# A decoder layer on one core: projections as three short passes, routed sums in DRAM, scatter in tiles of 128 rows

## What is computed

```python
# 1. mixer: running sums over the tokens
out = (a_b * c_b @ U_b.T + alpha * (a_t * z_t * c_t) @ U_t.T) / counts + bias;  x = x + out @ Wo.T
# 2. cross attention, 16 heads of 32 features
Q = x @ Wq.T                         # (224, 512)
K, V = split(ctx @ Wkv.T)            # two times (750, 512), contraction over 256
x = x + softmax(Q K.T * scale) V @ Wo.T
# 3. expert choice: 32 experts, each picks its 8 best tokens of every batch
vals, idx = top_k(softmax(x @ gate_w.T, over tokens), 8)
merged = sum_k x[idx_k] * vals_k                     # one row per batch and expert
o = gelu([merged, 1] @ w1[e]) ; o = [o, 1] @ w2[e]   # 512 -> 2048 -> 512
x = x.at[idx].add(o * vals)                          # scattered back to the tokens
```

## Time and profile before

| | us |
|---|---|
| three runs | 2379.69, 2379.73, 2370.84 (median 2379.69) |
| profiled execution | 2371.13 |
| its span | 2369.5 |
| TensorE busy | 1953.3 |
| VectorE busy | 974.9 |
| ScalarE busy | 754.6 |
| GpSimd busy | 826.8 |

### The profile page before, as it was taken

How to read it: one execution, slowest core, us unless ns; L and a number is a source line. 1 busy time by engine, 2 the same in 40 slices (tenths; PEclk the granted TensorE clock), 3 DMA queues, 4 the chain that set the end, 5 groups by cost and what they waited for, 6 DMA issues and landing times. The chain is left out here.

```text
span 2369.5 us, 39997 instructions
## 1 busy us (share of the span) xinstructions
PE 1953.3 (82%) x11970; PEld 1146.6 (48%) x11970; DVE 974.9 (41%) x2477; ACT 754.6 (32%) x1551; POOL 826.8 (35%) x592
## 2 busy tenths in 40 slices
PE   7789999999999999999999999986755655655633
PEld 5466666666666666666666666653211111111101
DVE  0355655656556556565565565651100000000003
ACT  2143434435444344354443443532100000000000
POOL 0245545555555455555554555543000000000000
PEclk8899999999999999999999999987877777777765
DMA  5223333242233332422433324263999999999974
GB/s 159 56 74 93 77 87 84 72 101 64 74 94 78 86 84 72 102 64 72 96 77 83 84 73 103 65 227 115 370 423 419 421 422 420 423 420 420 422 261 136
DMA packets 135414, 419.34 MB, mean 177 GB/s; under 512 B 32612, under 2 KB 74820, under 8 KB 110804
## 3 DMA queue, kind: packets, MB, share of 16 engines
q1 hardware_dynamic: 130292, 410.08, 50.9%
q10 hardware_dynamic: 4096, 7.80, 1.0%
q0 software_dynamic: 992, 1.02, 0.1%
HBM read 306.39 MB, written 16.15 MB: 136 GB/s over the span
## 5 line engine op out<-in xcount | busy, mean ns | idle before, releaser
L1035 DVE TENSOR_REDUCE maxes<-bank 112x1 f32<-112x376 f32 (+1 forms) x1024 | 506.8, 538 | 208.8 <-PE bank L1240 208.1
L863 ACT ACTIVATE probs<-bank 125x448 f32<-125x448 f32 x768 | 402.8, 546 | 360.4 <-PE bank L1262 353.2
L1262 PE MATMUL bank<-q_st,k_st 98*125 98x224 f32 x1536 | 384.3, 339 | 15.6 <-DMA q_st<-max_lo 9.1
L739 POOL TENSOR_TENSOR psum_keys<-psum_keys,probs 125x896 f32<-125x896 f32 x128 | 269.0, 2102 | 312.3 <-ACT probs L863 307.0
L1600 PE MATMUL bank<-ring,hid_T 128*32 128x512 f32 x1024 | 181.9, 875 | 204.3 <-DMA ring<-in_L_ffn_w 201.1
L1240 PE MATMUL bank<-k_st,q_st 96*112 96x376 f32 (+1 forms) x1024 | 324.7, 370 | 16.3 <-DVE maxes L1035 7.2
L1262 PEld LDWEIGHTS bank<-q_st,k_st 98*125 98x125 f32 x1536 | 265.6, 192 | 127.4 <-issue 74.7
L742 POOL TENSOR_TENSOR psum_keys<-psum_keys,probs 125x896 f32<-125x896 f32 x128 | 267.5, 2089 | 10.0
L1515 DVE TENSOR_TENSOR o_fin<-bank,b_row 16x512 f32<-16x512 f32 x32 | 21.7, 679 | 588.4 <-PE bank L1558 588.4
L1438 POOL DMA_DIRECT2D o_rows<-o_fin x31 | 15.3, 495 | 595.6 <-DVE o_fin L1515 595.6
L1240 PEld LDWEIGHTS bank<-k_st,q_st 96*112 96x112 f32 x1024 | 165.5, 180 | 80.5 <-DVE maxes L1035 45.4
(11 more groups left out here) (149 smaller groups left out, 2250.5 us busy)
## 6 DMA issues: line engine op xcount, KB each, us to landing
ring<-in_L_ffn_w SPq DMA_DIRECT2D x128, 2048.0 KB, 30.5
k_st<-k_hi SPq DMA_DIRECT2D x512, 93.8 KB, 2.2
k_st<-k_lo SPq DMA_DIRECT2D x256, 93.8 KB, 2.2
q_st<-q_hi SPq DMA_DIRECT2D x512, 28.0 KB, 1.8
ctx_nat<-in_ctx SPq DMA_DIRECT2D x16, 750.0 KB
x_in<-in_x SPq DMA_DIRECT2D x16, 448.0 KB, 3.6
q_st<-q_lo SPq DMA_DIRECT2D x256, 28.0 KB, 1.9
out<-x SPq DMA_DIRECT2D x16, 448.0 KB, 7.9
```

The lines of the kernel that those rows point to most:

```text
L739: nc.gpsimd.tensor_tensor(psum_keys[:], psum_keys[:], lo, ALU.add).then_inc(pool_chain, 1)
L863: nc.scalar.activation(probs[n % 2][:, j, :], bank[5 + u % 2][0:SK, 0:2 * T], ACT.Exp, scale=SCALE).then_inc(probs_ready, 1)
L1035: nc.vector.tensor_reduce(maxes[:, j, t, c:c + 1], bank[2 + n % 3][0:TT, 0:SC[c + 1] - SC[c]], AX.X, ALU.max).then_inc(s_drained, 1)
L1262: last = nc.tensor.matmul(bank[5 + u % 2][0:SK, kk * T:(kk + 1) * T], k_st[slot][:, j, k * SK:(k + 1) * SK], q_st[slot][:, j, :], start=Tr ...
```

## The change

1. *Projections.* Context and Wkv are kept as an fp32r tile with the rounded value and one with the rest: `wk_hi`, `wk_lo`, `wv_hi`, `wv_lo`, `ctx_hi`, `ctx_lo`. Each k and v job makes six fp32r matmuls (high by high, high by low, low by high, for two halves of the contraction) in place of two fp32 ones. `ctx_hi` is ScalarE's copy as before; `ctx_lo` is a new subtraction on VectorE, and it, not the copy, now frees the bank. In the setup VectorE makes four such subtractions, and TensorE waits for them before it reuses those banks.
2. *Routed sums.* `mt` turns 112 rows in place of 128; its result goes into a small tile `m_now` and is stored in `routed` in DRAM by one DMA per batch (`keep_routed`), and read back as one DMA at the end of the attention stage. `merged_T` and `b1_rows` now lie in the memory of V (`late`), so that the loads of the expert biases come later too, after the last multiplication by V. Some other tiles share memory.
3. *Scatter.* `out` is seen as 28 tiles of 128 rows. A tile may span two batches and then is the sum of two matmuls. `picks` is loaded by four DMAs, with zeros around each batch's columns. `o_rows` is read back in two parts: experts 0 to 15 before `out` is read, and 16 to 30 after the last weights. `out` is read by four DMAs of 128 partitions, and each tile is stored by a DMA of its own.

```diff
-                        nc.scalar.copy(ctx_T[:, kc, half * 3 * SK:(half + 1) * 3 * SK],
-                                       ps[:, 0:3 * SK]).then_inc(s, 1)
+                        nc.scalar.copy(ctx_hi[:, kc, half * 3 * SK:(half + 1) * 3 * SK],
+                                       ps[:, 0:3 * SK]).then_inc(ctx_hi_ready, 1)
...
+                    elif job[:2] == "ct":
+                        kc, cols = i % 2, slice(i // 2 * 3 * SK, (i // 2 + 1) * 3 * SK)
+                        dve.wait_ge(work_full, full)
+                        dve.wait_ge(ctx_hi_ready, bb * 4 + (i + 1))
+                        nc.vector.tensor_tensor(ctx_lo[:, kc, cols], ps[:, 0:3 * SK],
+                                                ctx_hi[:, kc, cols].bitcast(F32), ALU.subtract
+                                                ).then_inc(s, 1)
...
+                        terms = [(wk_hi, ctx_hi), (wk_hi, ctx_lo), (wk_lo, ctx_hi)]
                         for kc in range(KC):
-                            last = nc.tensor.matmul(ps[:, 0:SC[c + 1] - SC[c]],
-                                                    wk_T[:, kc, kt * P:(kt + 1) * P],
-                                                    ctx_T[:, kc, chunk(c)], start=(kc == 0),
-                                                    stop=(kc == KC - 1))
+                            for n, (w, z) in enumerate(terms):
+                                last = nc.tensor.matmul(ps[:, 0:SC[c + 1] - SC[c]],
+                                                        w[:, kc, kt * P:(kt + 1) * P],
+                                                        z[:, kc, chunk(c)],
+                                                        start=(kc == 0 and n == 0),
+                                                        stop=(kc == KC - 1 and n == 2))
...
+                def keep_routed(b):
+                    b = value(b)
+                    sp.wait_ge(mt_ready, b + 1)
+                    sp.dma_start(routed[b] if isint(b) else routed[bass.ds(b, 1)].rearrange(
+                        "o p n -> p (o n)"), m_now[:].rearrange("p k e -> p (k e)")
+                                 ).then_inc(m_stored, 16)
+
+                def recall_routed():
+
+                    sp.wait_ge(pv_done, 12 * B)
+                    expert_biases()
+                    sp.wait_ge(m_stored, 16 * B)
+                    sp.dma_start(merged_T[:, 0:LAST].rearrange("p b k e -> p b (k e)"),
+                                 routed[0:LAST].rearrange("b p n -> p b n")
+                                 ).then_inc(routed_loaded, 16)
...
                         if kt == 3 and kind != "first":
                             keep_weight(b - 1)
+                        if kt == 3 and kind != "first":
+                            keep_routed(b - 1)
...
-                for b in range(B):
-                    if b % RW == 0:
-                        sp.wait_ge(h_full if b < B // 2 else o_full, E - 1)
-                    sp.dma_start(fin(b), out[b, :, :].rearrange("(p t) d -> p t d", p=TT)
-                                 ).then_inc(fin_loaded[b // RW], 16)
+                sp.wait_ge(o_stored, 16 * (E - 4))
+                for r in range(RW):
+                    read_back(r, 0, E // 2)
+                for g in range(-(-NT // PER)):
+                    sp.wait_ge(h_full if g < 2 else o_full, E - 1)
+                    n = min(PER, NT - g * PER)
+                    sp.dma_start(ring[:, g, 0:n * D].rearrange("p (k d) -> p k d", d=D),
+                                 rows_out[:, g * PER:g * PER + n, :]).then_inc(fin_loaded[g], 16)
                 weights(end, 1, False, (2, 3))
                 sp.wait_ge(o_stored, 16 * (E - 1))
                 for r in range(RW):
-                    sp.dma_start(o_in[r * E:(r + 1) * E - 1, :, :],
-                                 o_rows.rearrange("(g r) e n -> r e g n", r=RW)[r, 0:E - 1, :, :]
-                                 ).then_inc(o_loaded, 16)
+                    read_back(r, E // 2, E - 1)
...
+                for cycle in range(GB):
+                    scatter(0, 0, True, True)
+                    scatter(1, 1, True, False)
+                    scatter(3, 2, True, False)
+                    scatter(5, 3, True, False)
+
+                    scatter(2, 1, True, True)
+                    scatter(4, 2, True, True)
+                    scatter(6, 3, True, True)
+
+                    scatter(1, 0, False, True)
+                    scatter(3, 1, False, True)
+                    scatter(5, 2, False, True)
```

More of the change, by code:

```diff
@@ L137, in build @@
         o_rows = nc.dram_tensor("o_rows", [B, E, D], F32).ap()
+        routed = nc.dram_tensor("routed", [B, P, KD * E], F32).ap()
         ident = sb(es, "ident", [P, P])
-        merged_T = sb(es, "merged_T", [P, KD, E, B])
-        b1_rows = sb(es, "b1_rows", [P, BANK])
+        late = sb(es, "late", [P, NK * D])
+        wv_lo = sb(es, "wv_lo", [P, KC, D], F32R)
+        merged_T = late[:, 0:B * KD * E].rearrange("p (b k e) -> p b k e", b=B, k=KD)
+        b1_rows = late[:, B * KD * E:B * KD * E + BANK]
         b1_loaded = sem("b1_loaded")
@@ L260, in build @@
             needs[len(flips)] = "kv"
-            for h, dst in ((0, wk_T), (1, wv_T)):
+            KV0 = len(flips)
+            kv_lo = []
+            for h, dst, lo in ((0, wk_hi, wk_lo), (1, wv_hi, wv_lo)):
                 for i in range(KC):
@@ L343, in _ @@
                     pe.wait_ge(s_out, n - 7)
+                    lo_taken(pe, n)
                     pe.wait_ge(s_cnt, 2)
@@ L1353, in build @@
         o_in = sb(es, "o_in", [P, GB, D])
-        picks = sb(es, "picks", [P, GB, T])
+        LEAD = [r * T % P for r in range(RW)]
+        picks = sb(es, "picks", [P, GB, LEAD[1] + T + 64])
         b1_flipped = sem("b1_flipped")
@@ L1377, in build, with fin, drained, tile_at @@
         fin_stored = sem("fin_stored")
-        def fin(b):
-            return ring[0:TT, b // RW, b % RW * 2 * D:(b % RW + 1) * 2 * D].rearrange(
-                "p (t n) -> p t n", t=2)
+        NT = B * T // P
+        PER = 2 * H // D
+        rows_out = out.rearrange("b t d -> (b t) d").rearrange("(k p) d -> p k d", p=P)
+        def fin(k):
+            return ring[:, k // PER, k % PER * D:(k % PER + 1) * D]
+        CYCLE = RW * T // P
+        TURN = [0, 2, 4, 6, 1, 3, 5]
+        def drained(k):
+            return k // CYCLE * CYCLE + TURN.index(k % CYCLE) + 1
+        def tile_at(n):
+            return n // CYCLE * CYCLE + TURN[n % CYCLE]
         with nc.Block() as block:
@@ L1414, in _, with read_back @@
                 weights(end, 1, False, (0, 1))
-                for b in range(B):
-                    if b % RW == 0:
-                        sp.wait_ge(h_full if b < B // 2 else o_full, E - 1)
-                    sp.dma_start(fin(b), out[b, :, :].rearrange("(p t) d -> p t d", p=TT)
-                                 ).then_inc(fin_loaded[b // RW], 16)
+                def read_back(r, e0, e1):
+                    sp.dma_start(o_in[r * E + e0:r * E + e1, :, :],
+                                 o_rows.rearrange("(g r) e n -> r e g n", r=RW)[r, e0:e1, :, :]
+                                 ).then_inc(o_loaded, 16)
+                sp.wait_ge(o_stored, 16 * (E - 4))
+                for r in range(RW):
+                    read_back(r, 0, E // 2)
[4 more added lines that the diff above has]
+                                 rows_out[:, g * PER:g * PER + n, :]).then_inc(fin_loaded[g], 16)
                 weights(end, 1, False, (2, 3))
@@ L1469, in _ @@
                     hidden(i, 1, False)
-                for b in range(B):
-                    act.wait_ge(fin_ready, 2 * b + 2)
-                    act.dma_start(out[b, :, :].rearrange("(p t) d -> p t d", p=TT), fin(b)
-                                  ).then_inc(fin_stored, 16)
-                act.wait_ge(fin_stored, 16 * B)
+                for n in range(NT):
+                    k = tile_at(n)
+                    act.wait_ge(fin_ready, n + 1)
+                    act.dma_start(rows_out[:, k, :], fin(k)).then_inc(fin_stored, 16)
+                act.wait_ge(fin_stored, 16 * NT)
             @block.vector
@@ L1611, in _, with scatter @@
                 sum_parts(E // 2 - 1, 1, False)
-                pe.wait_ge(picks_loaded, 16)
-                pe.wait_ge(o_loaded, 16 * (RW + GB))
-                for g in range(GB):
-                    for t in range(2):
-                        for r in range(RW):
-                            if g:
-                                pe.wait_ge(fin_ready, (g - 1) * 2 * RW + 2 * r + t + 1)
-                            rows = slice(r * E, (r + 1) * E)
-                            nc.tensor.matmul(bank[t * RW + r][0:TT, :],
-                                             tokens(picks[rows, g, :], t), o_in[rows, g, :],
-                                             start=True, stop=True).then_inc(scat_full, 1)
+                pe.wait_ge(picks_loaded, 16 * RW)
```

(14 more changed lines are left out.)

110 lines of the change are left out of this document (68 added, 42 removed).

## The result

The changed kernel takes 2406.77 us (median of four runs, 2405.45 to 2415.48); the kernel before, run beside it on the same chip, 2379.09 us. The ratio of the means of the runs is 1.0132, with a 95% interval of 1.0099 to 1.0165 (that of the two medians is 1.0116): slower by 1.3%, against 1.007 forecast (2397 over 2379.7). The profiled execution took 2405.45 us, with a span of 2403.8 us and a mean granted clock of 0.893.

The account below looks back on a forecast made before the run. It took SyncE's queue (q0 to xt0), then TensorE, to bound attention batches, with DMA and a one-engine read-back later. 2371.1 +31 +9 +1 -1 +15 -2.6 -27 -3 gave 2393; half the run spread made 2397 us, range 2375 to 2420.

Parts of the forecast that it names:

- signs: Listed trace marks, among them batches of 97 to 98 us, longer x_in waits, clock under 1.00, scatter 13 us after weights.
- The clock: Attention batches: TensorE falls to 1.2 GHz after waits, two falls in five batches, 1 us a batch, +15 us (0 to 39).
- rival 3: Attention batches: the clock falls in every batch for its full price, 2417 us, up to 2440; chance 0.15.
- ctx low parts: Context transposes: ct2 waits for VectorE's subtraction of ct0, 2.06 us a batch, 15 times, +31 us.
- The routed store: SyncE's queue ahead of load_x: one more DMA a batch, 0.65 us, 14 times, +9 us.
- The short passes: Key and value jobs, q0 to xt0: 72 us less TensorE time, costed at zero gain.
- SyncE's queue: Attention batch, first copy after q0 to xt0: queue of copies and loads sets 55.9 us, TensorE almost equal.
- Rival 1: Attention batches: TensorE is the bound after all, so the passes' 72 us come in, 2306 us; chance 0.17.
- Read-back: End: o_rows' second half on 15 partitions spreads over engines, scatter 13 us after weights, not 40.2; -27 us.
- the scatter: End: 28 adds in place of 32 and faster, earlier stores, -3 us (0 to -5).
- Rival 4: End: transfers to 15 partitions stay on one engine, +14, 2407 to 2411 us; chance 0.06.
- Reading `out`: Late stage: 128-partition reads 5.6 us less, o_rows ahead of the last weights 2.9 more, -2.6 us (-5 to +3).

Follow-up runs that it names:

- fp32_again: Changed kernel with each key and value job back to one fp32 product of the high parts, low parts still computed; 2395.6 us.
- fp32_no_ct_low: Changed kernel without the context's low parts, each key and value job one fp32 product of the high parts; 2350.2 us.
- no_ct_low: Changed kernel without VectorE's subtractions for the context's low parts; the second short pass takes the high part again; 2349.2 us.
- x_early_no_ct_low: Changed kernel with the load of x early and without the context's low parts, the high part's product added twice; 2309.8 us.
- raw_first: Changed kernel, arithmetic kept, ScalarE first copying the first context transpose's whole bank to SBUF to free it early; 2377.3 us.
- one_pass: Changed kernel with one short pass (high by high) in each key and value job instead of three; 2452.2 us.
- raw_x_early: Changed kernel, arithmetic kept, with the first context bank freed early through a copy and the load of x early; 2330.4 us.

## Why the prediction was right or wrong

**Verdict and size.** 2397 was said and 2406.8 measured, slower with a chance of 0.54. Against its own base, 2371.1 + 22 = 2393 was the sum and 2405.4 the execution: 12 us short, nearly all of it in the attention stage (+55 said, +65.7 measured); the end was -33 said and -31.4 measured. Of the signs that the prediction named for being right, all came but one: the batch is 98.75 us, not 97 to 98.

**The clock: the term that was mis-sized.** "I take 1 us a batch, two falls in five batches: +15 us, since some of the low clock will lie where TensorE waits anyway." Frequency and place were wrong. They came at the ct2 wait, in the stretch that TensorE paces, in eleven of twelve batches. The batch without one took 97.0 us, the other seven of the eight in the window 99.0 on average, so a fall costs 2.0 us, and all of them some 25 to 30 us in place of 15 (the sum, which had 15, is 12 short). That is rival 3's condition ("if each batch has a fall in its dense stretch, behind xt0"), and the time lies between the forecast and that rival. The price of "up to 2.6 us" came out near that by luck. Of the 2.6 us between the two batches that it was read from the earlier trace rows, 1.05 were busy time and 1.55 idle time, so most of it was the wait and not the clock; and the fall in that batch was 3.4 us long, not 6.8.

**ctx low parts.** 2.06 us a batch said. The wait is 2.26 us, and a batch with no fall took 97.0 us in the changed kernel and in fp32_again, where fp32_no_ct_low takes 95.05: 2.0. Right. With its clock the low part costs 57 us, from no_ct_low, where 31 + 15 = 46 was said.

**The routed store.** 0.65 a batch said; 0.49 is what fp32_no_ct_low takes above the kernel before (95.05 against 94.56), which no run puts down to the store alone. Right within the bounds.

**The short passes.** A record of 376 columns follows another after 0.17 us and one of 512 after 0.23, as the timeline shows, so a k job is 0.23 us shorter and a v job 0.33: 61 us in all, where I had 72. Costing it at zero came true: 1 us between no_ct_low and fp32_no_ct_low. In the changed kernel itself it is worse than zero, by 8 to 11 us (fp32_again), which I did not foresee: with short passes the falls were longer and more frequent.

**The step that failed in its reasoning.** "So 1024.47 to 1080.35 (55.9 us) is set by SyncE's queue, with TensorE almost equal to it". Removing the queue's last link gained nothing before the change, so it was TensorE that set the stretch, with the queue right behind. How close it was, two timelines and a run let one estimate: from the router's store to the load of x SyncE takes 1.65 us where it took 1.10, so the routed store is 0.55 us more of queue, and fp32_no_ct_low's batch is 0.49 us longer; if that is the store, the queue had hardly 0.1 us to spare. With two bounds so close, removing either one alone gives nothing: the short passes alone 1 us, the early load alone 0; together 2.2 us a batch. The forecast had this term right for a reason that was half right, and that is luck in part; a reader of "almost equal" should have asked which of the two gives way.

**Rival 1** (TensorE is the bound after all, 2306) named the true bound of the kernel before, but drew the wrong conclusion that its time would come in. It needs the early load of x. That x_early_no_ct_low came out near its figure, at 2309.8, is chance: the 2306 has 31 us for the low parts in it, which that run leaves out, and 72 us for passes of which 30 came in.

**Read-back.** Said was that 15 partitions spread and that "the scatter starts 13 us after the weights, not 40.2": 12.2 measured (2366.09 to 2378.27), and four transfers to 15 partitions took 1.78 us of the queue where four to 31 took 41.23. In the window from 2365 to 2372 DMA moves 12 GB/s, so nothing is left of a transfer at 25. Rival 4 is out. The rule of the Trainium skill that the prediction weighed ("DMA: Bandwidth & Descriptors", Why a DMA increments its semaphore by 16 and not by 1) gives one engine for 31 partitions and 15 for 15; the first agrees with 25 GB/s, and of the second the trace shows that the transfers spread, not over how many. *Reading `out`* in 128 partitions ran at 329 GB/s against 288 in one window each, but the -2.6 us did not come: the last weights land 654.7 us after the last `gate`, where it was 653.5, so 1.2 more. From the scatter to the end it takes 25.5 us where it took 30.1, 4.6 less, with 3 said.

Still open: why the clock falls in some batches at the wait for x_in and not in others (five of ten in raw_first, three of twelve in the changed kernel), why the last batch of attention comes in two lengths, and how much of before's rate of reading `out` is chance.

## What to carry over

When two resources are within a per cent of each other, relieving one may show nothing where relieving both shows a gain (here 0, 1 and 30 us); undo the suspected bound in the kernel *before* as well as after, since only that pair tells which one was there. Work taken away from TensorE in front of a wait can cost more than it saves: in one_pass the wait grew to 7.2 us and the clock was low over the work behind it. An extra drain on an engine that works in program order costs not its own 0.55 us but what stands in its queue ahead of it too, here 2.3 us of TensorE's time.

## What the runs showed of the hardware

- Less work for TensorE made the kernel slower: 11 us a batch out, 45 us more in all (one_pass), with TensorE at 1.2 GHz for about 26 of 102 us a batch, in stretches that begin at waits of 2 to 7 us.
- A wait of 2.26 us in otherwise dense work was followed by 6.8 us at 1.2 GHz in ten of twelve batches of the changed kernel; the wait of 1.93 us at `k3.1` had a fall in three of them. Batches whose waits stay under 1 us (before, raw_x_early) held 2.4 GHz in all eight.
- Four transfers to 15 partitions each were issued in 1.78 us, where four to 31 partitions held the queue for 41.23 us, at 25 GB/s.
